# First attention layer rebuilt by batch with 32-row score tiles, and stacked low-rank rows in the third feed-forward

## What is computed

```python
# L0 attention: 32 query heads of 16, 8 key/value heads of 16
q = (layernorm(x) @ Wq).reshape(8, 128, 32, 16)      # Wq 512x512
k = repeat((ctx @ Wk).reshape(8, 128, 8, 16), 4)     # Wk 512x128, each head serves 4 query heads
v = repeat((ctx @ Wv).reshape(8, 128, 8, 16), 4)
p = softmax(q k^T / 4)
x = x + tanh(g) * ((p v).reshape(8, 128, 512) @ Wo)
...
# F2: three projections, each with a low-rank part of rank 16 (512 -> 1376 -> 512)
def matmul_lora(x, w, a, b): return x @ w.T + (x @ a.T) @ b.T
hidden = silu(matmul_lora(x, gate)) * matmul_lora(x, up)
x = x + tanh(g) * matmul_lora(hidden, down)
```

## Time and profile before

| | us |
|---|---|
| median of 3 runs | 3003.39 (3002.08 to 3007.03) |
| the profiled execution | 2998.09 |
| its span, first to last instruction | 2996.1 |
| L0: first matmul to last output matmul | 8.3 to 296.6 |
| F0: first matmul | 298.45 |
| F2: its 11 tiles and their tail, to the first matmul of L3 | 1998.6 to 2227.6 |

### The profile page before, as it was taken

How to read it: one execution, slowest core, us unless ns; L and a number is a source line. 1 busy time by engine, 2 the same in 40 slices (tenths; PEclk the granted TensorE clock), 3 DMA queues, 4 the chain that set the end, 5 groups by cost and what they waited for, 6 DMA issues and landing times.

```text
span 2996.1 us, 47997 instructions
## 1 busy us (share of the span) xinstructions
PE 2846.4 (95%) x14914; PEld 2368.0 (79%) x14914; DVE 1788.6 (60%) x4181; ACT 1094.7 (37%) x3288; POOL 898.2 (30%) x780
## 2 busy tenths in 40 slices
PE   7997799999999999888999999989999999999998
PEld 5665588888888888667888888878877888888887
DVE  5666754465455446675777777744452555555557
ACT  4564233333333333123444444421113444444442
POOL 5433144243334324232222222235432222222210
PEclk9999999999999999999999999999999999999999
DMA  3000011011111111011000011111111000001000
GB/s 130 15 4 19 20 46 43 25 56 35 39 39 46 37 30 50 22 47 29 29 29 29 29 32 32 29 36 53 50 46 46 25 29 26 25 27 29 25 8 29
DMA packets 55235, 104.40 MB, mean 35 GB/s; under 512 B 6672, under 2 KB 6928, under 8 KB 54928
## 3 DMA queue, kind: packets, MB, share of 16 engines
q1 hardware_dynamic: 51840, 94.39, 10.8%
q10 hardware_dynamic: 3216, 7.81, 0.7%
HBM read 100.09 MB, written 2.10 MB: 34 GB/s over the span
## 4 chain that ended last, share of the span: by engine, by line
PE 85%; DVE 9%; ACT 3%; issue 3%; ACTq 0%; DVEq 0%
PE proj L578 38%; PE outp L578 22%; PE score L578 12%; PE value L578 9%; PE turned L807 4%; ACT probs L1232 2%; DVE top L1589 1%; DVE stats L1383 1%; DVE xt_lo L1412 1%; DVE x L1530 0%; DVE probs L1597 0%; DVE nt L1355 0%; PE turned L625 0%; DVE vz L1479 0%; DVE probs L1407 0%
## 5 line engine op out<-in xcount | busy, mean ns | idle before, releaser
L527 POOL TENSOR_TENSOR w_hi<-raw,zero 128x512 fp32r<-128x512 f32 x352 | 377.3, 1072 | 1793.3 <-PE proj L578 633.9
L1530 DVE SCALAR_TENSOR_TENSOR x<-outp,g_inv,x 128x512 f32<-128x512 f32 x768 | 556.4, 748 | 380.9 <-PE outp L578 379.9
L531 POOL TENSOR_TENSOR w_lo<-raw,w_hi 128x512 fp32r<-128x512 f32 x352 | 455.5, 1294 | 27.6
L578 PE MATMUL proj<-xt_hi,w_lo 128*128 128x512 f32 x928 | 394.6, 425 | 9.3 <-DVE xt_lo L1412 4.8
L578 PE MATMUL proj<-xt_hi,w_hi 128*128 128x512 f32 x928 | 368.4, 397 | 0.0
L578 PE MATMUL proj<-xt_lo,w_hi 128*128 128x512 f32 x928 | 366.1, 395 | 0.0
L578 PE MATMUL outp<-w_hi,a_lo 128*128 128x512 f32 x800 | 330.7, 413 | 30.5 <-DVE a_lo L1649 22.7
L578 PE MATMUL outp<-w_hi,a_hi 128*128 128x512 f32 x800 | 315.6, 394 | 0.0
L578 PE MATMUL outp<-w_lo,a_hi 128*128 128x512 f32 x800 | 314.8, 394 | 0.0
L1102 ACT ACTIVATE pT<-turned 128x512 f32<-128x512 f32 x320 | 192.0, 600 | 288.3 <-PE turned L807 288.3
L1232 ACT ACTIVATE probs<-probs,top 128x128 f32<-128x128 f32 x512 | 199.6, 391 | 238.6 <-DVE top L1573 126.8
(11 more groups left out here) (245 smaller groups left out, 5080.7 us busy)
## 6 DMA issues: line engine op xcount, KB each, us to landing
raw<-in_stream SPq DMA_DIRECT2D x352, 256.0 KB, 2.6
ctx_raw<-in_ctx_t ACTq DMA_DIRECT2D x4, 512.0 KB, 6.0
x<-in_x_in ACTq DMA_DIRECT2D x2, 1024.0 KB, 12.1
pb<-in_position_bias ACTq DMA_DIRECT2D x1, 2048.0 KB, 9.3
out<-x SPq DMA_DIRECT2D x8, 256.0 KB, 2.0
qw<-in_qweight ACTq DMA_DIRECT2D x1, 768.0 KB, 3.9
ln_w<-in_ln_weight ACTq DMA_DIRECT2D x1, 256.0 KB, 2.8
q_bi<-in_q_bias ACTq DMA_DIRECT2D x1, 256.0 KB, 2.6
```

What stands on the lines that cost most here:

```text
L527: pool.tensor_tensor(w_hi[:, k, :], raw[:, k % RAW, :], zero[:, :].to_broadcast([P, D]), ALU.add)\
L531: pool.tensor_tensor(w_lo[:, k, :], raw[:, k % RAW, :], f32(w_hi[:, k, :]), ALU.subtract)\
L578: m = pe.matmul(out_, l, r, start=start, stop=stop, skip_group_check=True)
L1530: dve.scalar_tensor_tensor(out=x[:, b, :], in0=O[no_f(k) % 2][:, :], scalar=scale, in1=x[:, b, :], op0=ALU.mult, op1=ALU.add)\
```

## The change

**L0** is written anew (`narrow_heads`, chunk table `Narrow`). It runs by batch: 8 batches of 4 units, each unit 8 heads, 32 units in all.
- The key projection has 128 columns instead of 512. ACT packs its weights out of four chunks (`wk_hi`, `wk_lo`, 8 copies). All query columns are projected ahead of the units or in the first two.
- DVE clears `kz` (8192 elements a partition) and fills `va` with ones (1088) first of all. SP then lays the keys into `kz` by 32 DMAs of 16 rows, between the tenth weight chunk and the next.
- Scores: 4 matmuls with 32 rows and 256 columns each, one for each 32 rows of the array, into the four banks of the new tile `four`; 8 heads at once.
- Softmax: DVE takes 8 maxima and subtracts them (128x1024, into one of three buffers), ACT does one exponential of 128x1024. The sum comes out of the value matmul: `va` has 17 columns for each head, the last of ones; stationary is now `pT`, moving is `va`.
- DVE divides by it (`normed`), 4 transposes turn the result (`attended_turn`), and 12 matmuls do the whole output of a batch. Its chunks are numbers 10 to 13, held until the last batch.
- The position bias of L1 is loaded at the start of F0 instead of at the start.

**F2**: the low-rank rows stand in four copies (hi and lo of the weights by hi and lo of the activations), put there by ACT (`lora_rows`), so that one matmul takes the place of the two of `stacked`, two take the place of three in `down_low`, and the last low-rank matmul of each batch is added inside `down` of the last tile.

```diff
-ATT = [Attention("L0", 4, 16, 0), Attention("L1", HEADS, 2, 8),
+ATT = [Narrow(), Attention("L1", HEADS, 2, 8),
...
+            sp.wait_ge(AS[0]["cleared"], 1)
+            sp.wait_ge(AS[0]["j_out"], 4)
+            for r in range(4):
+                for a in range(4):
+                    for odd in range(2):
...
+                        sp.dma_start(A0["kz"][row:row + 16, r, :, odd * P:(odd + 1) * P],
...
+                def scores(u):
+
+                    b, r = u // 4, u % 4
+                    pe.wait_ge(s["j_out"], 8 if b < B // 2 else 12)
+                    pe.wait_ge(kz_in[min(r, 1)], (24 if r else 8) * 16)
+                    if u:
+                        pe.wait_ge(s["sub"], u)
+                    for a in range(4):
+                        rows = slice(32 * a, 32 * a + 32)
+                        m = mm(four_banks[a][:, 0:2 * P], buf["qT"][rows, r, tokens(b)],
+                               buf["kz"][rows, r, b, :], True, True)
...
+                for k in range(L.steps):
+                    if k < L.UNITS:
+                        scores(k)
+                    if k < 2:
+                        query_piece(2 * k, 1)
+                        query_piece(2 * k + 1, 1)
+                    if L.UNITS <= k < L.UNITS + 2:
+                        early(1, k - L.UNITS)
+                    g, b = 2 * (k - 2), (k - 7) // 4
+                    if 0 <= g < 2 * L.UNITS:
+                        turn(g)
+                    if 1 <= g <= 2 * L.UNITS:
+                        values(g - 1)
+                    if k >= 7 and k % 4 == 3 and b < B:
+                        attended_turn(b)
+                    if 0 <= g < 2 * L.UNITS:
+                        turn(g + 1)
+                        values(g)
+                    if k >= 8 and k % 4 in (0, 1):
+                        output((k - 8) // 4, k % 4)
...
+                dve.memset(buf["kz"][:, :, :, :], 0.0).then_inc(s["cleared"], 1)
+                dve.memset(buf["va"][:, :, :, :], 1.0).then_inc(s["cleared"], 1)
...
-                    stacked(dst, ring(lora, tokens(w)), M2["low"][:, half(t)], True, True, False)
...
+                    pe.wait_ge(s["lora"], j + 2)
+                    mm(dst, w_hi[:, lora % RING, tokens(w)], M2["low"][:, half(t)], False, True)\
+                        .then_inc(s["proj"], 1)
...
-                        m = mm3(TV[t][:, :], ring(lora, tokens(2)), h, j == 0, last, last)
+                        m = mm(TV[t][:, :], w, M2["h_lo"][:, j % 2, half(t)], False, last)
...
-                add_tiles(HIDDEN_TILES, range(B))
```

More of the change, by code:

```diff
@@ L51 @@
 RAW = 2
+SPLIT_FIRST = 10
 RING = 8
@@ L54, with __init__, early_chunks @@
 MASKED = 1e30
-EARLY = {"L0": 0, "L1": 4, "L2": 8, "L3": 8}
+EARLY = {"L1": 4, "L2": 8, "L3": 8}
+class Narrow:
+    def __init__(self):
+        self.name = "L0"
+        self.UNITS = 4 * B
+        self.keys = [("v0", 0)] + [("k", r) for r in range(4)] + [("q", r) for r in range(4)]
+        self.order = self.keys + [("o", r) for r in range(4)]
+        self.chunk = {c: n for n, c in enumerate(self.order)}
+        self.pieces = [("v", 0, t) for t in range(2)] + [("k", 0, t) for t in range(2)]
+        self.pieces += [("q", r, t) for t in range(2) for r in range(4)]
+        self.evac = {what: n + 1 for n, what in enumerate(self.pieces)}
+        self.tile = {(0, b): b + 1 for b in range(B)}
+        self.steps = 4 * B + 6
+    def early_chunks(self):
+        return []
 class Attention:
@@ L267, in stream_order @@
             if n == 0:
-                order[-1:-1] = early
+                order = [(L.name, c) for c in L.keys] + early + [(L.name, ("o", r)) for r in range(4)]
             else:
@@ L702, in first_piece @@
                     else:
-                        c = chunk(lambda i: ((kind if kind == "v0" else kind[0]), h), 0, None)
-                        if kind == "v0" and part == 0:
-                            for kt in range(KT):
-                                pe.wait_ge(ctx_hi_done, kt + 1)
-                                pe.wait_ge(ctx_done, kt + 1)
-                                m = by_feature(dst(what), c, which, part, [kt], last=kt == KT - 1)
-                        else:
-                            m = by_feature(dst(what), c, which, part, last=True)
-                        m.then_inc(s["proj"], 1)
+                        c = chunk(lambda i: (kind[0], h), 0, None)
+                        by_feature(dst(what), c, which, part, last=True).then_inc(s["proj"], 1)
                         if part == 1 and kind != "Kc":
@@ L1001, in swiglu @@
                 pe.wait_ge(AS[3]["j_out"], ATT[3].early)
-                def stacked(dst, weights, low, weights_stand, start, stop):
-                    for no, w in enumerate(weights):
-                        l, r = (w, low) if weights_stand else (low, w)
-                        m = mm(dst, l, r, start and no == 0, stop and no == 1)
-                        if not (stop and no == 1):
-                            told(m)
-                    return m
                 def gate_or_up(j, t, w):
@@ L1162, in leave_bank @@
                         dst = buf["kT"][:, h % 2, half(part)]
-                    elif kind == "v0":
-                        dst = buf["vT"][:, half(part)]
                     elif kind == "v":
@@ L1292, in swiglu @@
                 phase_start(act, norm)
+                c = CHUNK_AT[("F2", ("A",))]
+                act.wait_ge(w_done, c + 1)
+                for w in (w_hi, w_lo):
+                    rows = w[:, c % RING, :].rearrange("p (k f) -> p k f", k=KT)
+                    o = copy(rows[:, :, 64:128], rows[:, :, 0:64])
+                o.then_inc(s["lora"], 1)
                 for kind, i in NORM_ORDER[2]:
@@ L1658, in attention @@
                 run_steps(dve, L, step)
-                if n == 0:
-                    behind(L.steps, None)
             def rms_scale(s):
@@ L1822, in swiglu, with low_parts @@
                 norm_all(norm)
-                def low_parts(what, banks, hi_done, lo_done):
+                def low_parts(what, banks, hi_done, lo_done, starts):
                     for t in range(2):
                         dve.wait_ge(s[hi_done], t + 1)
-                        rows = M2[what][32:64, half(t)]
-                        dve.tensor_tensor(rows, banks[t][32:64, :], f32(rows), ALU.subtract)\
-                            .then_inc(s[lo_done], 1)
+                        for r in starts:
+                            rows = M2[what][r:r + 32, half(t)]
+                            o = dve.tensor_tensor(rows, banks[t][r:r + 32, :], f32(rows), ALU.subtract)
+                        o.then_inc(s[lo_done], 1)
                 def hidden(j, t):
```

502 lines of the change are left out of this document (315 added, 187 removed).

## The result

The changed kernel takes 2909.88 us (median of 4 runs, 2899.76 to 2922.44), where the kernel before takes 3004.99 us beside it: a ratio of 0.9686 (95% interval 0.964 to 0.9732). The forecast was 2920 in a range of 2892 to 2955. The profiled execution has a span of 2920.6 us against 2996.1, so 75.5 us less; the forecast for it was 83.1 less.

A forecast was written before the change was run, and what follows sets the result against it. TensorE, busy 95% of the span, was taken as the bound. L0's 66.2 less 3.4 for a new wait plus F2's 20.3 gave 83.1 us: 2915 profiled, 2920 as median, range 2892 to 2955.

The forecast's parts named there:

- F2, tiles: F2's 11 tiles: 66 fewer matmuls at 0.230 us gain 15.2 us, with 0.8 lost at the first pair of copies.
- F2, tail: End of F2: 8 tiles of 4 matmuls with 8 additions, last addition at 2221.7 instead of 2227.6, gain 5.9 us.
- L0, start: Before L0's regular units: clears, weight copies, query pieces and first scores; units start at 66 us (62 to 72).
- The key DMAs: Start of L0: SP issues 32 at 0.43 us each, 14 us from about 34, hidden behind other work.
- L0, a unit: Each L0 unit on TensorE: scores 1.07, other work 3.47, waits 0.25, together 4.8 us.
- The scores: Four score matmuls of an L0 unit: only neighbouring tiles overlap in pairs, 5 steps of 0.21 us, 1.07 in all.
- The 0.25 for waits: In each L0 unit: waits and changes of form add some 0.25 us to TensorE's work.
- rival 1: L0 units: scores do not overlap, or DVE's subtraction makes the cover too thin; 20 us more, 2941; chance 0.33.
- Rival 2: L0 units: all four score tiles run at once, DVE holds the unit at 4.15 us; 2899; chance 0.15.
- L0, end: After L0's last unit: 20.4 us to the last output matmul, at 230.4 instead of 296.6, gain 66.2 us.
- The new wait: Start of F0: chunks held until L0's last output delay POOL's splits, so TensorE waits 3.4 us (2 to 5).
- Rival 3: L0 units: gaps keep the clock at 1.2 GHz, C = 9.3 us, 3064; chance 0.05, with what lies beyond 3000.

The follow-up runs named there:

- after_again: The changed kernel run and profiled once more with nothing changed: 2903.97 us, profiled span 2901.6 us.
- all_rows: The changed kernel with each of a unit's four score matmuls on all 128 rows of the array instead of 32: 2932.59 us, ratio 0.9761.
- chunk_waits: The changed kernel, with value pieces waiting for each weight chunk right ahead of its own matmuls, not for the last of four first: 2901.32 us.
- same_rows: The changed kernel with all four score matmuls of a unit on rows 0 to 31 of the array: 3070.66 us, ratio 1.0235.
- spread: The changed kernel with the four late query pieces spread over the first seven units instead of two, with other banks: 2903.24 us, ratio 0.9668.

## Why the prediction was right, step by step

- **F2, tiles.** 15.2 less 0.8 were forecast, 17.1 came (216.4 to 199.3 us from the norm wait to the last `down_low`). A tile lost 1.55 us for 6 matmuls, 0.26 each and not 0.230: the 80 that are left are a little faster too (18.25 / 80 = 0.228, before 19.81 / 86 = 0.230). The copies on ACT are hidden, as said.
- **F2, tail.** 5.9 forecast, 3.7 measured. The step that failed is the wait and the clock: TensorE waits 1.24 and 0.34 us there, and then runs eight matmuls at half the clock (0.43 instead of 0.23, 2139.99 to 2143.36), 1.6 us. F2 in all: 20.3 forecast, 20.8 measured, so the two errors, 2.7 and 2.2, nearly cancel.
- **L0, start.** Regular units at 66 forecast, 67.85 in the profile (65.87 in `after_again`). The memsets of `kz` and `va` take 7.8 us, not 8.3, but DVE begins them at 2.52 us only, so the first matmul comes at 11.77 instead of about 10.5, the norm transposes at 32.90 instead of 32. The key DMAs were mis-sized: SP issues the 32 in 21.70 us from 33.78 on, 0.68 each and not 0.43. They cost nothing all the same, since the second unit's scores stand at 61.54 and wait for nothing.
- **L0, a unit.** 4.8 forecast. 30 steps from 67.85 to 209.6 make 4.73; without the half clock the mean is 4.12 (`after_again`), and the six steps that it struck take 6.2 to 8.9. The scores were mis-sized: 0.65 and not 1.07. The argument that the second record of a tile must follow the first and so only pairs overlap is wrong. The 0.25 for waits was nothing. With them the forecast's sum is 3.47 + 0.65 = 4.12, the mean at full clock. That it is equal to 0.01 is luck: a batch with its output takes 4.26 a unit, 0.14 more than the sum, and the first six of these units carry none. The Trainium skill's figure of 3.07x for four tiles of 32 rows (TensorE: Matmul & The Clock Gate, Part 3) gave an estimated 0.56 and was nearer than my own count; against the 1.81 of `all_rows` the trace has 2.8x. The drain at a change of tiling mode, which the Trainium skill states (TensorEngine Tiling (Array Packing), Key Properties) and on which rival 1 drew, has no row of its own. By an estimate from the rows it must fit into what the 0.65 has over the 0.45 of one such matmul (a quarter of 1.81): 0.2 us at most for a group.
- **DVE.** It never holds a unit at full clock: TensorE has one wait of 0.80 us between 65 and 190 us in `after_again`, and that is for ACT. There the maximum takes 1.21 to 1.23 us and the subtraction 1.23, not 1.7; in the last of the rows below it is DVE that waits for the scores. So both causes of rival 1 are out. Rival 2 was right on the scores and near with its 4.15 for the unit, but by luck: it had DVE set that time, and TensorE sets it.

```profile
118.33 1.21 DVE L1599 TENSOR_REDUCE top<-four 128x8 f32<-128x1024 f32 x1
119.57 1.23 DVE L1604 TENSOR_TENSOR shifted<-four,top 128x1024 f32<-128x1024 f32 x1
...
121.90 1.23 DVE L1599 TENSOR_REDUCE top<-four 128x8 f32<-128x1024 f32 x1 [0.51 <-PE four L583]
```

- **L0, end.** 20.4 forecast, 20.3 (209.6 to 229.93). Last output matmul at 230.4 forecast, 229.93 in the profile, 209.57 in `after_again`. The gain is 66.3 against 66.2, which is luck: the sum had units too slow by 30 x 0.68 = 20 and left out 18.4 of half clock.
- **The new wait.** The mechanism was right, 3.4 too small. POOL ends 9.3 us after the output's first matmul (236.6 against 227.31), not 8.0: it starts 1.7 later than that matmul and waits once for a load (0.48). TensorE would have gone on at about 232.7 (2.35 behind the end of the last output matmul, as in `chunk_waits`), so 4.1 for the wait. The step that failed is the clock behind it, which the forecast did not have: 2.5 us more. With it the norm transposes of F0 come 7.1 us later than before, the logits 8.0. The 6.42 us of idle time are one value of several: it is 4.83 to 7.88 over the nine profiles with this wait.
- **Rival 3**, the clock at 1.2 GHz through all units and a time of 3064, got a chance of 0.05. Its half clock is what `same_rows` shows (3070.66), and for the units from 71 to 111 us what the changed kernel shows. Its cause, gaps on TensorE, is not there, and what was said against it, that the units are fuller than before, did not keep the clock up: TensorE was busy for 41.87 of 42.00 us at a clock of 0.52.

What the forecast lacked is thus a term of 0 or 18 us. With it and the right scores, it would have been 2900 or 2918, near where the nine runs are. Its range of 2892 to 2955 holds both.

## What to carry to other kernels

Small f32 matmuls on four different 32-row groups run side by side: count four of them (32 rows, 256 columns) as about one and a half of one, and don't put them on one row group behind each other, which cost 160 us here. When a change takes the wide matmuls out of a loop, read the granted clock of that loop, and in more than one execution: one profile can hide or invent 18 us. Moving wide work into such a loop, as `spread` does, cost nothing here, and none of its three profiles has the half clock in these units; that it prevents it is not shown. When weights are held to the end of a stage, let the next stage wait for each chunk by itself.

## What the runs showed of the hardware

- Four f32 matmuls of 32 rows and 256 columns on four row groups take 0.65 us together at full clock; one after the other they take 1.92 on one row group and 1.81 on all rows.
- A loop of such matmuls on one row group, with transposes and narrow value matmuls, ran at a granted clock of 0.55 from 90 to 340 us while TensorE was never idle. The same loop with all 128 rows in the same places ran at 1.00.
- An f32 matmul with a stationary operand of 128x128 costs about 0.23 us at 17 columns and 0.01 more at 128.
- The same program can get half the clock for some 41 us of its units in one run (0.52 from 70 to 112 us) and none of it there in another (1.00), with first scores that start 2 us apart.
